# Loading the last stage's weights and first images in the stage ahead, and storing the last images in pieces

## The reference

```
x = shortcut + attention(layer_norm(x))
y = layer_norm(x)
y = conv3x3(y, w_ffn1) * bn1_scale + bn1_shift      # 48 -> 192 channels
y = gelu(y)
y = conv1x1(y, w_ffn2) * bn2_scale + bn2_shift      # 192 -> 48 channels
return x + y
```

## Time and profile before

| | us |
|---|---|
| median of 3 runs | 2753.61 |
| lowest and highest | 2752.81, 2753.72 |
| profiled execution | 2749.97 |
| its span, first to last instruction | 2748.1 |

### The profile page before, as it was taken

One profiled execution on the slowest core, in us unless ns is written; L12 is line 12 of the kernel. 1 busy time (PEld: TensorE's weight loads), 2 busy tenths in 40 slices (PEclk: granted clock), 3 DMA queues, 4 the chain that ended last, 5 costly groups with the idle time before them and its releaser, 6 DMA issues. The chain is left out here.

```text
span 2748.1 us, 97903 instructions
## 1 busy us (share of the span) xinstructions
PE 2591.1 (94%) x35944; PEld 1602.9 (58%) x35944; DVE 2302.6 (84%) x3650; ACT 2092.1 (76%) x3862; POOL 2022.9 (74%) x2134
## 2 busy tenths in 40 slices
PE   6888599999999999999999999997699999999998
PEld 2333266666666666666666666664466666666665
DVE  1222389999999999999999999995699999999997
ACT  2444388888888888888888888885577777777775
POOL 0222367777777777777777777774799999999996
PEclk9999699999999999999999999998899999999999
DMA  5552311221221211211211212212998887988871
GB/s 150 142 142 72 95 40 47 52 51 46 53 51 47 53 50 47 53 49 48 53 49 49 53 48 50 53 46 52 166 158 140 146 148 130 153 137 146 148 115 36
DMA packets 235602, 231.14 MB, mean 84 GB/s; under 512 B 117808, under 2 KB 230448, under 8 KB 232368
## 3 DMA queue, kind: packets, MB, share of 16 engines
q1 hardware_dynamic: 235440, 228.95, 41.1%
HBM read 151.07 MB, written 77.76 MB: 83 GB/s over the span
## 5 line engine op out<-in xcount | busy, mean ns | idle before, releaser
L634 POOL TENSOR_TENSOR kex<-ks,cw 112x294 f32<-112x294 f32 x1024 | 778.5, 787 | 17.8 <-ACT ks L926 17.8
L628 POOL TENSOR_TENSOR s<-s,mx 113x588 f32<-113x588 f32 x256 | 300.7, 1175 | 357.7 <-DVE mx L1079 357.7
L1343 POOL TENSOR_TENSOR v<-ya 128x448 f32<-128x448 f32 x448 | 473.1, 1085 | 43.0 <-DMA ya<-y_chunks 22.0
L1072 DVE TENSOR_TENSOR s<-ps_s,bias 113x588 f32<-113x588 f32 x512 | 392.1, 766 | 82.0 <-PE ps_s L712 82.0
L724 PEld LDWEIGHTS ps_t<-cw,s 113*98 113x98 f32 x3072 | 288.0, 128 | 268.5 <-issue 228.1
L724 PE MATMUL ps_t<-cw,s 113*98 113x113 f32 x3072 | 398.1, 266 | 26.0 <-ACT pt L957 25.5
L1079 DVE TENSOR_REDUCE mx<-s 113x12 f32<-113x588 f32 x512 | 389.1, 760 | 8.9
L741 PEld LDWEIGHTS ps_o<-vs,pt 98*49 98x49 f32 x12288 | 302.4, 126 | 138.5 <-DVE on L1103 74.9
L712 PE MATMUL ps_s<-kex,q 48*49 48x294 f32 x4096 | 366.7, 424 | 1.2 <-issue 1.2
L950 ACT ACTIVATE s<-s 113x588 f32<-113x588 f32 x512 | 355.2, 694 | 1.9 <-POOL s L628 1.7
L957 ACT ACTIVATE pt<-ps_t 98x588 f32<-98x588 f32 x512 | 336.9, 658 | 18.1 <-PE ps_t L724 6.2
(11 more groups left out here) (168 smaller groups left out, 6089.9 us busy)
## 6 DMA issues: line engine op xcount, KB each, us to landing
ya<-y_chunks SPq DMA_DIRECT2D x64, 532.9 KB, 9.8
y_chunks<-y SPq DMA_DIRECT2D x256, 76.1 KB, 1.8
xin<-x_chunks SPq DMA_DIRECT2D x256, 73.5 KB, 2.5
xres<-x_chunks SPq DMA_DIRECT2D x256, 73.5 KB, 1.9
x_chunks<-xo SPq DMA_DIRECT2D x256, 73.5 KB, 1.8
out<-xr SPq DMA_DIRECT2D x32, 588.0 KB, 7.2
yb<-y_chunks SPq DMA_DIRECT2D x96, 177.6 KB, 11.3
xr<-x_chunks SPq DMA_DIRECT2D x32, 514.5 KB, 7.9
```

Of the source, the lines that this page charges most:

```text
L628: pool.tensor_tensor(by_head(s_sb[d]), by_head(s_sb[d]), mx[d][:, :, :].rearrange("q i h -> q (i h)").unsqueeze(2).to_broadcast([QP, 2 * H ...
L634: ins = pool.tensor_tensor(kex[a][:, win, :, :], ks[:, win, :].unsqueeze(1).to_broadcast([PP, HEADS, N]), w("head").unsqueeze(2).to_broadc ...
L1072: dve.tensor_tensor(s_sb[d][:, :, :], ps_s[0:QP, :, 0:HN], bias[:, low, int(d == DUOS - 1), :].unsqueeze(1).to_broadcast([QP, 2, HN]), ALU ...
L1343: pool.tensor_tensor(v[t % 2][:, term, :, :].rearrange("q a (r x) -> q a r x", r=R1), first, second, op).then_inc(v_set, 1)
```

## The change

An object `Ahead` holds tiles and semaphores that live longer than one stage: `cw2` for the whole program, and from the start of attention `cw3`, the pad values and one set of the last stage's tiles (`ya0`, `yb0`, `xr0`, for the even pairs).

- The attention weights are loaded in the first stage, between the loads of the first and the second group of images.
- In attention, SyncE loads `cw3` at chunk 0. At the end of chunk 1 VectorE makes the pad values and the border of `yb0`, at the end of chunk 2 GpSimd clears all of `xr0` and copies the border rows of `ya0`. At chunks 124 to 127 SyncE issues the loads of pair 0: 9 for `ya`, 9 for `ya`, 18 for `yb`, 6 for `xr`.
- The last stage loads pair 1 first. Only the second set of tiles is prepared there. The clearing of `ps_f` and of rows of `xr1` on VectorE stands behind `wmid` and ahead of `wa_hi`.
- The last pair is stored in three pieces: units 0 to 3, 4 and 5, and 6, with two DMAs each.

```diff
@@ layer0, SyncE @@
-            for k in range(2):
-                load(k, k)
+            load(0, 0)
+            sp.dma_start(ahead.cw2[:, :], ahead.pack2).then_inc(ahead.at_weights_in, 16)
+            load(1, 1)
...
@@ attention, SyncE @@
-            sp.dma_start(cw[:, :], pack).then_inc(weights_in, 16)
...
                     store_y(n - 3, 1 - a)
+                if isinstance(n, int):
+                    begin_last_stage(n)
+
+            def begin_last_stage(n):
+                first = CHUNKS - 2 * EDGE
+                done = (RC - 1) * pairs // 2 + 1
+                if n == 0:
+                    sp.dma_start(ahead.cw3[:, :], ahead.pack3).then_inc(ahead.ff_weights_in, 16)
+                if n == first:
+                    sp.wait_ge(y_out[0], done * 32)
+                    sp.wait_ge(ahead.ya_zeroed, 1)
+                if n == first + 2:
+                    sp.wait_ge(ahead.yb_zeroed, 1)
+                if n == first + 3:
+                    sp.wait_ge(x2_out[0], done * 32)
+                    sp.wait_ge(ahead.xr_zeroed, 1)
+                if n in (first, first + 1):
+                    load_ya(sp, ahead.ys, 0, n - first, ahead.ya, ahead.ya_in)
+                if n == first + 2:
+                    load_yb(sp, ahead.ys, 0, ahead.yb, ahead.yb_in)
+                if n == first + 3:
+                    load_xr(sp, ahead.x2s, 0, ahead.xr, ahead.x2_in)
...
@@ attention, GpSimd @@
                     shift(n, 3)
+                if isinstance(n, int) and n == 2:
+                    pool.wait_ge(ahead.pad_ready, 1)
+                    pool.memset(ahead.xr[:, :], 0.0).then_inc(ahead.xr_zeroed, 1)
+                    for img in range(2):
+                        for row in (0, H - 1):
+                            ins = pool.tensor_copy(ahead.ya[:, img, row * YW:(row + 1) * YW], ahead.pad[:, 0:1].to_broadcast([128, YW]))
+                    ins.then_inc(ahead.ya_zeroed, 1)
...
@@ attention, VectorE @@
                     row_max(n, 3)
+                if isinstance(n, int) and n == 1:
+                    dve.wait_ge(ahead.ff_weights_in, 16)
+                    dve.tensor_scalar(ahead.pad[:, 0:1], PACK3.at(ahead.cw3, "be_a"), -1.0, None, op0=ALU.mult)
+                    dve.tensor_scalar(ahead.pad[0:PP, 1:2], PACK3.at(ahead.cw3, "be_b"), -1.0, None,
+                                      op0=ALU.mult).then_inc(ahead.pad_ready, 1)
+                    dve.wait_ge(ahead.pad_ready, 1)
+                    dve.tensor_copy(ahead.yb[:, (H - 1) * YW - 2:], ahead.pad[0:PP, 1:2].to_broadcast(
+                        [PP, YW + 2])).then_inc(ahead.yb_zeroed, 1)
...
@@ feed_forward, SyncE @@
-            sp.dma_start(cw[:, :], pack).then_inc(weights_in, 16)
...
             sp.wait_ge(ya_zeroed, 1)
-            load_ya(0, 0)
+            load_y(1, 1)
             sp.wait_ge(yb_zeroed, 1)
-            load_yb(0, 0)
+            load_yb(sp, ys, 1, yb[1], yb_in[1])
             sp.wait_ge(xr_zeroed, 1)
-            load_x(0, 0)
-            load_ya(1, 1)
-            load_yb(1, 1)
-            load_x(1, 1)
+            load_xr(sp, x2s, 1, xr[1], x2_in[1])
...
-                sp.wait_ge(result, units)
-                for a in range(2):
-                    sp.dma_start(out[pair * 2 + a, :, :], xr[b][BO * a:BO * a + C, :]).then_inc(out_done[b], 16)
+                for first, end in LAST_PIECES if pair == DUPLES - 1 else ((0, C1),):
+                    part_of = slice(first * T1, end * T1)
+                    sp.wait_ge(result, pair * C1 + end)
+                    for a in range(2):
+                        sp.dma_start(out[pair * 2 + a, :, part_of], xr[b][BO * a:BO * a + C, part_of]).then_inc(out_done[b], 16)
...
@@ feed_forward, GpSimd @@
-            pool.wait_ge(pad_ready, 1)
-            for b in range(2):
-                for a in range(2):
-                    for row in (0, H - 1):
-                        ins = pool.tensor_copy(ya[b][:, a, row * YW:(row + 1) * YW], pad[:, 0:1].to_broadcast([128, YW]))
+            for a in range(2):
+                for row in (0, H - 1):
+                    ins = pool.tensor_copy(ya[1][:, a, row * YW:(row + 1) * YW], pad[:, 0:1].to_broadcast([128, YW]))
             ins.then_inc(ya_zeroed, 1)
...
@@ feed_forward, VectorE @@
-            dve.wait_ge(weights_in, 16)
-            dve.tensor_scalar(pad[:, 0:1], w("be_a"), -1.0, None, op0=ALU.mult)
-            dve.tensor_scalar(pad[0:PP, 1:2], w("be_b"), -1.0, None, op0=ALU.mult).then_inc(pad_ready, 1)
-            dve.wait_ge(pad_ready, 1)
-            for b in range(2):
-                ins = dve.tensor_copy(yb[b][:, (H - 1) * YW - 2:], pad[0:PP, 1:2].to_broadcast([PP, YW + 2]))
-            ins.then_inc(yb_zeroed, 1)
-            for b in range(2):
-                ins = dve.memset(xr[b][BO // 2:BO, :], 0.0)
-            ins.then_inc(xr_zeroed, 1)
-            dve.memset(ps_f[BO // 2:BO, :, :], 0.0).then_inc(f_rows_set, 1)
+            dve.tensor_copy(yb[1][:, (H - 1) * YW - 2:], pad[0:PP, 1:2].to_broadcast([PP, YW + 2])).then_inc(yb_zeroed, 1)
             dve.wait_ge(beta_mm, 1)
...
                 dve.tensor_scalar(wmid[k][:, :], wmid[k][:, :], 0.5, None, op0=ALU.mult).then_inc(wmid_set, 1)
+            dve.memset(ps_f[BO // 2:BO, :, :], 0.0).then_inc(f_rows_set, 1)
+            dve.memset(xr[1][BO // 2:BO, :], 0.0).then_inc(xr_zeroed, 1)
```

More of the change, by code:

```diff
@@ L91, with layer0 @@
 })
-def layer0(nc, x, pack, x1s):
+def layer0(nc, x, pack, x1s, ahead):
     ctx = ExitStack()
@@ L446, in _, with attention @@
                 add(GROUPS - 1, 1, p)
-def attention(nc, x1s, pack, x2s, ys):
+def attention(nc, x1s, x2s, ys, ahead):
     ctx = ExitStack()
@@ L1161, in _, with load_rows, load_ya, load_yb @@
             each_chunk(body)
-def feed_forward(nc, x2s, ys, pack, out):
+REST = 128 - 2 * C
+Y_DMAS, X_DMAS, OUT_DMAS = 18, 6, 2
+def load_rows(sp, ys, pair, a, tile, first, channels, shift, move, signal):
+    count = channels.stop - channels.start
+    src = ys[:, pair, a * C + channels.start:a * C + channels.stop, :]
+    mid = (RC - 1) * WS
+    to = (SHIFT + 1 - shift) * YW - move
+    sp.dma_start(tile[first:first + count, to:to + mid * YW].rearrange("c (n t) -> c n t", n=RC - 1),
+                 src[0:RC - 1, :, :].rearrange("n c t -> c n t")).then_inc(signal, 16)
+    low = H - SHIFT - mid - (1 if shift == 0 else 0)
+    to += mid * YW
+    sp.dma_start(tile[first:first + count, to:to + low * YW], src[RC - 1, :, 0:low * YW]).then_inc(signal, 16)
+    skip = 1 if shift == 2 else 0
+    start = (H - SHIFT - mid + skip) * YW + move
+    size = (SHIFT - skip) * YW - move
+    to = (skip + 1 - shift) * YW
+    sp.dma_start(tile[first:first + count, to:to + size], src[RC - 1, :, start:start + size]).then_inc(signal, 16)
+def load_ya(sp, ys, pair, a, tile, signal):
+    load_rows(sp, ys, pair, a, tile[:, a, :], 0, slice(0, C), 0, 0, signal)
+    load_rows(sp, ys, pair, a, tile[:, a, :], C, slice(0, C), 1, 0, signal)
+    load_rows(sp, ys, pair, a, tile[:, a, :], 2 * C, slice(0, REST), 2, 0, signal)
+def load_yb(sp, ys, pair, tile, signal):
+    for a in range(2):
+        for kw in range(3):
+            load_rows(sp, ys, pair, a, tile, BO * a + kw * (C - REST), slice(REST, C), 2, kw, signal)
+def load_xr(sp, x2s, pair, tile, signal):
+    mid, edge = (RC - 1) * T2, SHIFT * W
+    for a in range(2):
+        rows = slice(BO * a, BO * a + C)
+        src = x2s[:, pair, a * C:(a + 1) * C, :]
+        sp.dma_start(tile[rows, edge:edge + mid].rearrange("c (n t) -> c n t", n=RC - 1),
+                     src[0:RC - 1, :, :].rearrange("n c t -> c n t")).then_inc(signal, 16)
+        sp.dma_start(tile[rows, edge + mid:HW], src[RC - 1, :, 0:T2 - edge]).then_inc(signal, 16)
+        sp.dma_start(tile[rows, 0:edge], src[RC - 1, :, T2 - edge:T2]).then_inc(signal, 16)
+def feed_forward(nc, x2s, ys, out, ahead):
     ctx = ExitStack()
@@ L1177, in sem @@
             return ctx.enter_context(nc.semaphore(name))
-        rest = 128 - 2 * C
         DUPLES = B // 2
@@ L1188, in feed_forward @@
         wmid = [sb(f"wmid{k}", [128, HID]) for k in range(2)]
[L1189 to L1191 removed]
+        ya = [ahead.ya, sb("ya1", [128, 2, H * YW])]
+        yb = [ahead.yb, sb("yb1", [PP, H * YW])]
+        xr = [ahead.xr, sb("xr1", [PP, HW])]
         wa_hi, wa_lo = sb("wa_hi", [128, 4, HA], F32R), sb("wa_lo", [128, 4, HA], F32R)
@@ L1251, in _ @@
         def _(sp):
-            sp.dma_start(cw[:, :], pack).then_inc(weights_in, 16)
-            def load_rows(pair, a, tile, first, channels, shift, move, signal):
-                count = channels.stop - channels.start
-                src = ys[:, pair, a * C + channels.start:a * C + channels.stop, :]
-                mid = (RC - 1) * WS
-                to = (SHIFT + 1 - shift) * YW - move
-                sp.dma_start(tile[first:first + count, to:to + mid * YW].rearrange("c (n t) -> c n t", n=RC - 1),
-                             src[0:RC - 1, :, :].rearrange("n c t -> c n t")).then_inc(signal, 16)
```

(18 more changed lines are left out.)

69 lines of the change are left out of this document (35 added, 34 removed).

## The result

The changed kernel takes 2731.87 us (median of 4 runs, 2727.25 to 2736.01) against 2753.66 in the same comparison: a ratio of 0.9917, with an interval of 0.9904 to 0.993. The forecast was 2729.0 with a range of 2725.5 to 2733.5. The same kernel compared once more gave 2729.36 (2726.37 to 2732.21), ratio 0.9915 [0.9898, 0.9933]. The profiled execution took 2733.26 us, a span of 2731.4.

The account below looks back on a forecast made before the run. TensorE, always busy in the attention and last-stage loops, was taken as the bound; only stretches between could shrink. 18.0 + 5.7 + 1.1 - 0.2 = 24.6 us off 2753.6 gave 2729.0 us, range 2725.5 to 2733.5.

Parts of the forecast that it names:

- The third rival: Last stage: pair 1 loads come late and TensorE waits at unit 7, giving 2747 us; chance 0.03.
- the second: End of attention: SyncE's issue queue stalls on the pair 0 loads; at 2 us per issue 2780 us; chance 0.03.
- Head: Last stage, first instruction to first product: 18.0 us saved, between 16.3 and 19.3.
- clearing of `xr`: Head of the last stage: VectorE's clearing, hidden before, is now on the path ahead of the weight split, 3.4 us.
- low parts, to the product: Head of the last stage: two low parts at 696 ns, 1.4 us, then 0.2 us until TensorE can begin.
- GpSimd beside it: Head of the last stage: VectorE slowed beside GpSimd, four operations charged at 1.3 us; bounds 0 and 3.0 us.
- the nine: Head's two-input VectorE operations (`wsum`, two `wmid`, four `wa_lo`, two low parts), each some 0.33 us more beside GpSimd.
- the first rival: Head of the last stage: GpSimd holds VectorE for whole instructions, 4.1 us instead of 1.3, giving 2731.8 us; chance 0.12.
- End: End of the program: storing the last pair in pieces shortens the last wait, 5.7 us saved.
- The bound of 4.5: End of the program: lower bound of the saving in us, if the 344 KB piece is still moving.
- Start of attention: Start of attention: weights already there, VectorE goes on at 309.3, 1.1 us saved; PSUM clearing is late next.
- Added to attention: Attention: new work costs 0.2 us in all; bounds 0 and 1 for added work, 0 and 1 for pair 0 loads.

Follow-up runs that it names:

- e7: The kernel of e5 with `xr0` cleared before GpSimd's wait for the pads and the attention weights loaded two groups later: 2731.91 us, ratio 0.9917.
- e9: The kernel of e8 with `xr0` cleared on GpSimd behind its wait for the pads, ahead of the chunk loop: 2724.08 us, ratio 0.9897.
- e5: The changed kernel with `ps_f` cleared ahead of VectorE's wait for the shift products and `xr1` behind the low parts of unit 0: 2728.37 us, ratio 0.9911.
- e8: The kernel of e5 with GpSimd waiting ahead of its low parts of unit 0 until the weights are split: 2727.58 us, ratio 0.9911.
- e2: The changed kernel with the attention weights loaded at the start of attention again: 2731.8 us, ratio 0.9922.
- e3: The kernel before the change with only its last pair stored in pieces: 2748.86 us, ratio 0.9982.
- e4: The changed kernel with pair 0 loaded at the start of the last stage again: 2739.54 us, ratio 0.9946.
- e1: The changed kernel compared again with no edit: 2729.36 us, ratio 0.9915.
- e6: The changed kernel with GpSimd waiting with the terms of unit 1 until the weights are split: 2727.44 us, ratio 0.9904.

## Why the prediction was right, step by step

**The bound and the loops.** The loop of the last stage stayed at 785.46 of 786 us with no idle TensorE. The third rival (loads too late) is out, and so is the second: SyncE's issues in the last four chunks took 0.42 to 0.46 us mostly, not 1.15. (The free time that I set against them was 4 x 8.6 = 34.4 us and not 33; it changes nothing.) From the first product to the last addition the profiles still differ by up to 2.4 us (791.30 in e7, 793.69 in e9). Some 1.0 us of that lies ahead of the first addition (20.49 and 21.45 us behind the first product), where the granted clock rises from 0.50 to 1.00 at different moments: in the stretch from 2 to 4 us behind the first product it is 0.76 in e7 and 0.50 in e9. The rest stays open.

**Head: 18.9 us against 18.0.** Its own steps, from 1920.84:

| step | predicted us | measured us |
|---|---|---|
| wait for the shift products | 4.0 | 4.04 |
| shifts, `wsum`, `wmid` | 1.77 | 1.73 |
| clearing of `ps_f` | 1.1 | 1.12 |
| clearing of `xr` | 3.4 | 3.41 |
| `wa_hi`, `wa_lo`, alone | 1.56 | 1.56 |
| low parts, to the product | 1.6 | 1.22 |
| GpSimd beside it | 1.3 | 0.86 |
| sum | 14.8 | 13.94 |

(In the last rows the split took 2.42 us in all; 0.86 over 1.56 is put down to GpSimd.) The order of steps and what is late next held, the uncovered clearing above all. Two terms were too large. The low parts took 0.58 us each and not 0.70. I had taken the 696 ns for a low part that runs alone, and that is a misreading: in the head of before GpSimd was at its transforms then, and the two took 0.65 and 0.74. In the changed kernel GpSimd idled beside them.

The other term, the 1.3 us beside GpSimd, had its size nearly right and its mechanism wrong. I had read the mean stretch of 0.33 us as a price per operation and kept the whole-instruction hold as a rival at 0.12. e5, e7 and e8 show the hold: casts of 1.03 us, multiplications of 2.4, and casts of 0.22 once GpSimd waits. And it hit the casts, which I had not counted among the nine, not the `wa_lo`. The changed kernel pays only 0.86 us because the clearing of `xr`, which only writes, ran for 2.67 us beside GpSimd's four transforms and left one of them over. The step that failed is the argument against the first rival, "the stretch is 0.33 us on average and not 1.0". The mean of 1022 ns is of two kinds: of the 224 low parts in before's trace 111 take 0.61 us on average, 110 take 1.44, and three lie between. VectorE's timeline of before's loop has one of each:

```profile
2300.82 1.44 DVE L1603 TENSOR_TENSOR v_lo<-v,v_hi 128x448 fp32r<-128x448 f32 x1
...
2303.19 0.61 DVE L1603 TENSOR_TENSOR v_lo<-v,v_hi 128x448 fp32r<-128x448 f32 x1
```

GpSimd's own first low part runs from 2300.64 to 2301.78 there, so VectorE's 1.44 us ends 0.5 us after it. All 110 long ones start inside a low part of GpSimd and end 0.5 us behind its end; the short ones start just as one ends. So a collision costs 0.83 us and not 0.33, and half of the low parts pay it. The mean hid this, though the trace of before held it.

By its price the first rival (first product 2.8 us later) did not come; by its mechanism it was right, and for e5 I expected a head of 9.4 to 10.3 us from my own rule and got 13.25.

The Trainium skill describes this (SBUF — State Buffer, Who interferes with whom): copy, cast and tensor_scalar can use VectorE's two-port modes, then contend with GpSimd, and the one that starts first holds the pair for its whole instruction; order decides, not shape. The rows agree: 2.42 us for a tensor_scalar under a 2.71 us GpSimd clearing, and 1.03 against 0.23 us for a cast.

**End: 5.8 us against 5.7.** The nearest row, the 1.8 us of the 76 KB stores, was the right one: 84 KB landed in 1.9. In the changed kernel landing takes 1.9, 2.3, 4.0 and 7.1 us for 84, 168, 336 and 588 KB, and the last one alone is waited for. The Trainium skill's rule for large transfers (DMA: Bandwidth & Descriptors, Bandwidth), weighed in the prediction, is not contradicted for bandwidth (588 KB in 7.1 us are more per microsecond than 84 KB in 1.9), but it would have kept the latency here. The bound of 4.5 (an earlier piece still moving) did not come true.

**Start of attention: 0.9 us against 1.1.** As predicted the clearing of PSUM is late next. e2 gives 1.09.

**Added to attention: charged 0.2, measured 0.9 to 1.5.** The clearing in chunk 2 costs 0.3 us (12.38 against 12.05 in e9). The pair-0 loads cost 0.6 to 1.2, at one place, and not for the reason that I gave their upper bound. At that place no store came late; TensorE's own queue stood still. One store did come late, further on: behind the 18 `yb` issues, which took 9.5 us where 8.6 were free, it left 1.24 us after its result was there (0.03 before). It cost nothing, since the next addition came 9.67 us behind the last one in both kernels. The two costs keep about within the bounds of 1 us each, but the value taken, 0.2 for all, was the mis-sized term.

The last step of attention varies from 4.5 to 6.1 us, and not by the change: it is 4.53 in before, 5.23 in e3 and 6.07 in e4, none of which has the early loads, and 4.53 to 5.93 in the others. It goes with the granted clock there, 1.00 in before, 0.82 in e3 and 0.59 in e4, where TensorE's products take 0.86 us instead of 0.49. At 5.76 us in the changed kernel's first profile it is most of the 1.52 us by which attention was longer.

**The sum.** 18.9 + 5.8 + 0.9 - 1.2 = 24.4 us by stages, where 24.6 was predicted. The medians give 21.8 and, with e1's runs, 25.0 (2754.31 - 2729.36). That the stages come within 0.2 us of the forecast is partly luck: the head gave 0.9 us more than forecast and what was added to attention cost 1.0 us more. By chance the first median, 2731.87, is also the number of the first rival (2731.8). The stages tell them apart: the rival has the head save 15.2 us, and it saved 18.9.

**The spread.** "The runs of before differ by 0.9 us" was wrong: with more runs before went from 2749.2 to 2758.9 us, the changed kernel from 2726.4 to 2736.0. Profiles put most of it on the first stage, 305.7 to 312.7 us, by how often the granted clock falls to 0.90 in it and by when the second batch of images is there. Single runs of the changed kernel cover 9.6 us, more than the 8 us of my range; their medians of four lie inside it. The range took nothing from the spread of runs but a wider low end, and that was too little.

## What to carry to other kernels

- Where VectorE prepares something short beside GpSimd, ask instruction by instruction which GpSimd instruction is running when it starts: it may wait for the rest of it. A mean over many instructions can hide this; look at the single durations. A wait on GpSimd's side, put where GpSimd has slack, took 3.7 us off the head with no work removed. Let clearings, and not casts or small multiplications, run beside GpSimd's arithmetic.
- When a load is taken off a path, list the work that it was hiding in program order, small clearings included; that list was the forecast. Then store the last result in pieces that shrink.
- One change of a microsecond is seen in the stretch where it acts, not in a median whose runs spread by several.

## What the runs showed of the hardware

- A VectorE cast or multiplication from SBUF to SBUF waited for a GpSimd instruction to end: 1.03 us instead of 0.23 beside GpSimd's low parts and transforms (e5), 2.42 instead of 0.38 (before) or 0.21 (changed kernel) under a clearing of 2.71 us (e7). VectorE's own clearing of `xr` kept its 2.67 us beside GpSimd (1928.44 in the changed kernel).
- A subtraction with both inputs in SBUF is held too: VectorE's low parts take 0.61 or 1.44 us in before's loop, about half of them each, 1.44 when they start inside a low part of GpSimd.
- The two hold each other: in e8 two low parts of VectorE took 2.09 us and those of GpSimd beside them 2.92, against 1.16 and 2.31 when apart.
- The granted clock in the first stage differs from run to run of one program, 0.90 or 0.98 in a stretch of 70 us; three such dips instead of one make about 5.5 of 7.0 us, and a later second batch of images the rest.
- At the start of the last stage the granted clock goes from 0.50 to 1.00 sooner or later from run to run (0.76 in e7, 0.50 in e9 in the stretch from 2 to 4 us behind the first product); the first addition then comes 1.0 us sooner or later.
- While the loads of pair 0 were moving, some 8 us behind the first of them, TensorE's weight loads stood still for 0.62 us with nothing to wait for (e6). Cause open.
